# One decoder layer on one core: maxima moved among the projections, layer norm and values on ScalarE, self attention's outputs kept on chip

## The reference

```
x = x + self_attention(layernorm(x))      # causal; values have a bias, the output projection too
x = x + cross_attention(layernorm(x), ctx, mask)   # ctx: (4, 77, 256)
x = x + down(silu(gate(n)) * up(n))       # n = layernorm(x); int32 weights times 1/127, 256 -> 768 -> 256
```

## Time and profile before

| | us |
|---|---|
| median of three runs | 1133.68 |
| the profiled execution | 1134.03 |
| span of its trace | 1132.3 |
| TensorE busy | 1044.6 (92%) |
| VectorE busy | 748.3 (66%) |
| ScalarE busy | 571.1 (50%) |
| GpSimd busy | 224.3 (20%) |
| mean granted TensorE clock | 0.961 of full |

### The profile page before, as it was taken

The page is one execution under the profiler, slowest core; times in us unless marked ns, Lnnn a source line. Parts: engine busy times, 40 slices in busy tenths (PEclk is TensorE's granted clock), DMA queues, the critical chain, the costliest instruction groups (busy, mean ns, idle before and its releaser), DMA issues. The chain is left out here.

```text
span 1132.3 us, 19037 instructions
## 1 busy us (share of the span) xinstructions
PE 1044.6 (92%) x7092; PEld 608.6 (54%) x7092; DVE 748.3 (66%) x1603; ACT 571.1 (50%) x1043; POOL 224.3 (20%) x191
## 2 busy tenths in 40 slices
PE   2888989999999999999999895689989899999997
PEld 2777434444444444444444463344444688888886
DVE  5999887777887887877786374356544555555552
ACT  1445147667776677677666664646646211111110
POOL 6545550000000000000000032600000133333331
PEclk9999779999999999999999996889989899999998
DMA  7259844333334444444020045848774211111101
GB/s 244 104 198 251 248 86 74 73 75 70 71 70 89 90 86 88 89 89 86 23 76 27 35 130 187 204 89 171 169 177 126 80 43 49 51 53 50 48 9 37
DMA packets 89811, 113.66 MB, mean 100 GB/s; under 512 B 13822, under 2 KB 74922, under 8 KB 88183
## 3 DMA queue, kind: packets, MB, share of 16 engines
q1 hardware_dynamic: 86071, 107.43, 38.3%
q10 hardware_dynamic: 3648, 5.02, 2.1%
HBM read 66.26 MB, written 45.45 MB: 99 GB/s over the span
## 5 line engine op out<-in xcount | busy, mean ns | idle before, releaser
L782 ACT ACTIVATE prob<-bank 128x512 f32<-128x512 f32 (+1 forms) x608 | 329.2, 575 | 180.2 <-PE bank L826 101.5
L734 DVE TENSOR_REDUCE pm<-bank 128x1 f32<-128x512 f32 (+3 forms) x608 | 364.3, 655 | 82.5 <-PE bank L810 62.0
L805 PE MATMUL bank<-stk,stq 96*128 96x512 bf16 (+3 forms) x768 | 226.6, 339 | 2.7 <-DVE pm L734 2.1
L822 PE MATMUL bank<-stq,stk 98*128 98x512 bf16 (+3 forms) x768 | 222.4, 328 | 0.9 <-ACT prob L782 0.8
L836 PE MATMUL bank<-prob,va 128*17 128x512 f32 (+3 forms) x1536 | 164.0, 500 | 0.0
L805 PEld LDWEIGHTS bank<-stk,stq 96*128 96x128 bf16 x768 | 70.1, 98 | 153.5 <-DVE pm L734 114.1
L1554 ACT ACTIVATE e_sg<-bank 128x512 f32<-128x512 f32 x48 | 28.7, 598 | 188.7 <-PE bank L135 188.7
L967 POOL TENSOR_TENSOR c_rstd<-c_ve,mhalf 128x4 f32<-128x4 f32 x8 | 8.1, 1010 | 521.3 <-DVE c_ve L128 521.3
L1311 ACT ACTIVATE xprob<-bank 80x512 f32<-80x512 f32 x128 | 72.3, 592 | 65.5 <-PE bank L1349 64.0
L822 PEld LDWEIGHTS bank<-stq,stk 98*128 98x128 bf16 x768 | 69.2, 98 | 56.7 <-issue 12.2
L810 PE MATMUL bank<-tri_q,identb 128*128 128x128 bf16 (+2 forms) x352 | 88.3, 251 | 0.0
(11 more groups left out here) (172 smaller groups left out, 1379.4 us busy)
## 6 DMA issues: line engine op xcount, KB each, us to landing
qk<-a_parts SPq DMA_DIRECT2D x32, 384.0 KB, 4.3
od<-u_out SPq DMA_DIRECT2D x16, 512.0 KB, 3.2
oin<-od SPq DMA_DIRECT2D x32, 256.0 KB
od<-xu SPq DMA_DIRECT2D x16, 512.0 KB, 3.9
xq<-c_parts SPq DMA_DIRECT2D x16, 384.0 KB, 2.9
xstq<-xq SPq DMA_DIRECT2D x32, 192.0 KB, 4.3
stq<-qk SPq DMA_DIRECT2D x28, 192.0 KB, 4.6
stk<-qk SPq DMA_DIRECT2D x14, 384.0 KB, 7.1
```

The costliest lines, as they stand in the source:

```text
L734: nc.vector.tensor_reduce(pm[:, k, h0:h0 + hb, r], src[:, 0:hb * w].rearrange("p (h w) -> p h w", h=hb), AX, ALU.max).then_inc(s_mxe, 1)
L782: nc.scalar.activation(prob[:, U % NPS, 0:hb * n], bank[STB[U % NSB]][:, 0:hb * n], ACT.Exp).then_inc(s_ex, 1)
L805: mm = nc.tensor.matmul(dst[:, h * w:(h + 1) * w], stq[i][0:R, half, h0 + h, r * P:(r + 1) * P], stk[i][0:R, h0 + h, k0:k0 + w], start=(h ...
L822: mm = nc.tensor.matmul(dst[:, h * n:(h + 1) * n], stk[i][0:RM, h0 + h, kt * P:(kt + 1) * P], stq[i][0:RM, half, h0 + h, q0:q0 + n], start ...
```

## The change

In the projections, layer norm moves to ScalarE (scale and a negated mean times scale as bias, which GpSimd computes), the values are evicted by ScalarE without bias into one bank, and the four products share three banks. The value bias goes through the output projection once and into the output bias. In each of chunks 4 to 7, seven units of group 0's maxima are placed among the products (28 of 39 in all, behind the places 0 to 5 that `LEAD_AT` counts), in two other banks. Groups 0 and 1 are loaded one chunk earlier.

In self attention the products of two sets stand together, with 16 buffers of exponentials instead of 12 and three buffers of queries, keys and values instead of four. Each group's outputs and denominators are stored by eight DMAs into tiles on chip (`oall`, `den`), and nothing is read back. In the middle stage these loads are gone, `load_later` comes first, and the feed-forward weights are loaded and converted during cross attention, in 12 pieces.

```diff
-        TB, QKB, VB = (0, 1), (2, 3, 4, 5), (6, 7)
+        TB, QKB, VB = (0, 1), (2, 3, 4), 5
 # SP, chunk(c)
-                if c in (3, 4):
+                if c in (2, 3):
...
+                if c == NCH - 2:
+                    self_rows(sp, 0, 0)
 # GpSimd
             nc.gpsimd.tensor_tensor(rstd[:, c % 2], ve[:, c % 2], mhalf[:], ALU.pow).then_inc(s_pow, 1)
+            g.wait_ge(s_pow, c + 1)
+            nc.gpsimd.tensor_tensor(negm[:, c % 2], mom[:, c % 2, 0], rstd[:, c % 2], ALU.mult).then_inc(s_nm, 1)
 # VectorE
-            normalise1(1)
+            nc.vector.tensor_copy(bvb[:], bv_c[:, :, None].to_broadcast([P, KT, P])).then_inc(s_bvb, 1)
+            lead = iter(range(NLEAD))
             for c in range(NCH):
+                at = LEAD_AT if c >= LEAD_FROM else (0,) * 6
                 split(c, 0)
+                for n in islice(lead, at[0]):
+                    self_item(v, 0, n)
                 split(c, 1)
+                for n in islice(lead, at[1]):
+                    self_item(v, 0, n)
+                if c + 2 < NCH:
+                    stats1(c + 2)
                 if c + 1 < NCH:
                     turned_low(c + 1)
-                if c + 2 < NCH:
-                    stats1(c + 2)
+                for n in islice(lead, at[2]):
+                    self_item(v, 0, n)
                 split(c, 2)
+                for n in islice(lead, at[3] + at[4]):
+                    self_item(v, 0, n)
                 split(c, 3)
-                if c + 2 < NCH:
-                    normalise1(c + 2)
...
+                for n in islice(lead, at[5]):
+                    self_item(v, 0, n)
+            v.wait_ge(s_bo, 1)
+            nc.vector.tensor_tensor(bo_b[:], bank[TB[0]][:, 0:D], bo_b[:], ALU.add).then_inc(s_bob, 1)
 # ScalarE
+            normalise1(1)
             for c in range(NCH):
                 high(c, 0)
                 high(c, 1)
                 middle(c, 0)
                 if c + 1 < NCH:
                     turned(c + 1)
+                middle(c, 1)
+                values_out(c, 0)
                 high(c, 2)
-                middle(c, 1)
+                middle(c, 2)
+                values_out(c, 1)
                 high(c, 3)
-                middle(c, 2)
                 middle(c, 3)
+                if c + 2 < NCH:
+                    normalise1(c + 2)
 # TensorE
+                product(c, 0)
+                for n in islice(lead, at[0]):
+                    self_maxima(t, 0, n)
+                product(c, 1)
...
+                if c + 1 < NCH:
+                    turn(c + 1)
                 values(c, 0)
...
+                product(c, 2)
...
                 values(c, 1)
...
+                product(c, 3)
+                for n in islice(lead, at[5]):
+                    self_maxima(t, 0, n)
 # self attention
-        NPS, LAG, LATE = 12, 3, 3
+        joint_end = [sets[s - s % 2 + 1][3] for s in range(len(sets))]
+        NPS, LAG, LATE = 16, 3, 3
+        LDB = (6, 7)
+        LEAD_FROM, LEAD_AT = 4, (1, 1, 1, 1, 1, 2)
-            plan += [("p", s, 0) for s, x in enumerate(sets) if x[3] - 1 == u - LAG]
+            plan += [("p", s, 0) for s in range(len(sets)) if joint_end[s] - 1 == u - LAG]
 # SP
             def store(g):
+                b, i = g // GB, g % GB
                 sp.wait_ge(s_u, 2 * g + 2)
-                sp.dma_start(od[g:g + 1].rearrange("a h w r t -> (a h w r) t"), u_out[:, g % 2]).then_inc(us[g % 2], 16)
+                for h in range(HG):
+                    row = HD * (HG * (i % 2) + h)
+                    sp.dma_start(oall[row:row + HD, b, i // 2],
+                                 u_out[h * VW:h * VW + HD, g % 2]).then_inc(us[g % 2], 16)
+                    row = S // DT * (HG * i + h)
+                    sp.dma_start(den[row:row + S // DT, b],
+                                 u_out[h * VW + HD:h * VW + VC, g % 2]
+                                 .rearrange("a (c t) -> a c t", t=DT)).then_inc(us[g % 2], 16)
-            for i in range(2, GB):
+            for i in range(2, NB):
                 a.wait_ge(s_set, i + 1)
                 load_self(a, i)
 # middle, SP
-            load_den(sp, B - 1)
-            load_outputs(sp, 3)
-            load_outputs(sp, 4)
+            load_later(sp)
+            store_shares(sp, B - 1)
+            load_shares(sp, B - 1)
             for c in range(NCH):
-                if c + 5 < NCH:
-                    load_outputs(sp, c + 5)
                 for n in range(KT):
                     store_queries(c, n)
-                if c == 0:
-                    store_shares(sp, B - 1)
-                    load_shares(sp, B - 1)
-                    load_later(sp)
-                if c == 4:
-                    load_last_weight(sp)
 # middle, VectorE
+            shares(v, B - 1)
             for k in range(KT):
                 quotients(v, 3, k)
 # middle, ScalarE (and GpSimd's low part likewise)
-                if 3 <= c < 6:
-                    ffn_weight_high(a, c - 3)
 # cross attention, SP
+                if g < 2:
+                    load_weight(sp, g)
+                if g == 6:
+                    load_weight(sp, 2)
 # cross attention, ScalarE
+                    if u == NST2 - 2 and 1 <= g <= 3 * NPC:
+                        ffn_weight_high(a, g - 1)
```

More of the change, by code:

```diff
@@ L1 @@
 from contextlib import ExitStack
+from itertools import islice
 import concourse.bass as bass
@@ L557, in qkv_tensor, with product @@
             t.wait_ge(s_a, 2)
+            def product(c, n):
+                need(t, s_r, 4 * c + n - 2)
+                if c == 0 and n == KT:
+                    t.wait_ge(s_kl, 2)
+                w_ = (wq, wk)[n // KT]
+                m = cut_products(bank[QKB[(4 * c + n) % 3]][:],
+                                 [(w_[:, :, k, (n % KT) * P:(n % KT + 1) * P], xnt[:, c % 2, :, k]) for k in range(KT)])
+                m.then_inc(s_qk, 1)
+            lead = iter(range(NLEAD))
             for c in range(NCH):
+                at = LEAD_AT if c >= LEAD_FROM else (0,) * 6
@@ new lines, in qkv_tensor @@
+                product(c, 2)
+                for n in islice(lead, at[3]):
+                    self_maxima(t, 0, n)
+                values(c, 1)
+                for n in islice(lead, at[4]):
+                    self_maxima(t, 0, n)
+                product(c, 3)
+                for n in islice(lead, at[5]):
+                    self_maxima(t, 0, n)
+            t.wait_ge(s_xt, KT * NCH)
+            t.wait_ge(s_bvb, 1)
+            t.wait_ge(s_later, 16 * 4)
+            for k in range(KT):
+                m = nc.tensor.matmul(bank[TB[0]][:, 0:D], bvb[:, k], wo[:, k], start=(k == 0), stop=(k == KT - 1))
@@ new lines, in self_maxima @@
+        def self_maxima(t, g, n):
+            i, N = g % NB, g * NMX + n
+            kind, m = ring[n]
+            dst = mx_bank(N)
+            if n == 0:
+                t.wait_ge(ld[i], 16 * NLD * (g // NB + 1))
+            need(t, s_mxe, N + 1 - (len(LDB) if g == 0 else NMB))
+            if kind == "t":
+                t.wait_ge(s_mt, 2 * g + m + 1)
+                nc.tensor.transpose(dst[0:32, 0:P // 2].bitcast(BF16),
+                                    mt[:, m].rearrange("p t m -> p (t m)"), identb[:]).then_inc(s_mxf, 1)
+                return
+            half, k, r, h0, hb, k0, w, diag = mx_units[m]
+            for h in range(hb):
+                mm = nc.tensor.matmul(dst[:, h * w:(h + 1) * w],
+                                      stq[i][0:R, half, h0 + h, r * P:(r + 1) * P],
+                                      stk[i][0:R, h0 + h, k0:k0 + w],
+                                      start=(h == 0), stop=not diag, skip_group_check=True)
+            if diag:
+                mm = nc.tensor.matmul(dst[:, 0:hb * w].rearrange("p (h w) -> p h w", h=hb)[:, :, w - P:w],
+                                      identb[:], tri_q[:, 0:hb], start=False, stop=True, skip_group_check=True)
+            mm.then_inc(s_mxf, 1)
@@ L859, in self_tensor @@
                     elif what == "r" and g + ahead < G:
-                        maxima(g + ahead, which)
-            for s, x in enumerate(sets):
-                if x[3] - 1 > NST - 1 - LAG:
+                        self_maxima(t, g + ahead, which)
+            for s in range(len(sets)):
+                if joint_end[s] - 1 > NST - 1 - LAG:
                     products(G - 1, s)
-        ldo = sems("c_ldo", 3)
-        s_den = sem("c_den")
         s_rd = sem("c_rd")
```

326 lines of the change are left out of this document (149 added, 177 removed).

## The result

The changed kernel took 1129.66 us (median of 16 runs) beside 1138.65 us (16 runs) of the kernel before: ratio 0.9928, 95% interval 0.9905 to 0.9952. It is faster, but the forecast was 1099, and the range 1082 to 1118 missed it. The profiled execution took 1128.56 us, its trace spans 1126.8 (before 1132.3). The two traces so differ by 5.4 us where the medians differ by 9.0: the profiled run of the kernel before, at 1134.03, was one of its quicker ones. The table explains the 5.4.

| stretch, from ...

A forecast was written before the change was run, and what follows sets the result against it. It took VectorE to bound the projections, TensorE self attention, and no engine the middle stage. Start +3, self attention -17, middle -23.5 and cross attention +3 made -34.5 us, giving 1099 us, range 1082 to 1118.

The forecast's parts named there:

- -16.6, -4.3 and -2.6: Middle stage: output reads gone -16.6, last chunk's shorter wait -4.3, its products off the low clock -2.6; sum -23.5 us.
- a gain or a loss of 2 is within the bounds: Entry of the middle stage: nothing taken, as quotients wait for eight small stores and shares instead of a store and reads.
- wrong if the middle keeps a wait over 5 us: Middle stage: a sign that would prove the prediction wrong; no wait for outputs was expected there.
- Self attention: -17: Self attention: fewer visits to column tiles save 22 us, banks take back 5; -17 us (-22 to 0).
- The price of a visit: Self attention: going to the column tiles and back costs 0.23 us; 6 visits a group instead of 12 save 1.4 us.
- I take 0.3 us a group: Self attention: loss while eight products run and neither VectorE nor ScalarE gets a bank; 0.3 us a group, 5 us overall.
- The start: +3: Projections up to the first exponentials and group 1's small instructions: +3 us (-6 to +12), last product at 134.0.
- 1.3 us of bounds 0 to 6: Projections, chunk 4: its wait for group 0's load, asked for one chunk earlier behind chunk 2's stores; 1.3 us (0 to 6).
- the same loss that group 0 to 1 has now: Start of self attention: later bias additions meet group 1's small VectorE instructions; two at 2.26 us and the wait, less slack.
- Ten issues at the pitch of rows 5: Before the first exponential: ScalarE's ten DMA issues for group 2 stand ahead of it in its queue; about 5.0 us.
- Rival B: Projections lose more through load and hand-offs: +15 us for +3, giving 1111; chance 0.12.
- Cross attention: +3: Cross attention: twelve weight pieces on ScalarE about nothing, GpSimd idle, three weight loads 1 us each; +3 us (0 to +8).

The follow-up runs named there:

- Experiment 2: Changed kernel, with the last group's eight stores issued first in the middle stage and the last batch element's shares computed after chunk 0's splits: 1121.63 us, ratio 0.9868.
- experiment 1: Changed kernel, with each set's products on their own again, 12 visits to the column tiles per group instead of 6: 1137.72 us, ratio 0.9987.
- experiment 11: Changed kernel, with self attention's products in four visits to the column tiles a group instead of six: 1119.58 us, ratio 0.9842.
- experiment 4: Changed kernel, with chunk 4's seven maxima at later places, none before the second product's transposes: 1130.43 us, ratio 0.9918.
- experiment 13: Changed kernel, with GpSimd's eight bias additions waiting for the last small VectorE casts of groups 0 to 3, two each: 1127.71 us, ratio 0.9902.
- Experiment 14: Changed kernel, with GpSimd's quotients of chunk 0 after its tenth weight piece and group 12's casts, chunk 1's after group 14's casts: 1120.04 us, ratio 0.9851.
- kernel 12: Changed kernel, with last stores in the middle stage, chunk 4's maxima later, GpSimd's bias additions and quotients placed, and four visits a group: 1094.44 us, ratio 0.9621.
- Kernel 10: Changed kernel, with last stores in the middle stage, chunk 4's maxima later, and GpSimd's bias additions and quotients placed by waits on casts: 1108.92 us, ratio 0.9754.
- experiment 5: Changed kernel, with GpSimd's quotients of cross attention and its eight output bias additions cut into quarters: 1132.01 us, ratio 0.9937.
- experiment 3: Changed kernel, with none of group 0's maxima among the projections' products, all 39 following the last product: 1138.98 us, ratio 1.0005.

## Why the prediction was wrong

The forecast's gain of 34.5 us was 9.0 in the medians and 5.4 in the traces. Four terms failed, and self attention's was the largest.

**Middle stage: right.** -16.6, -4.3 and -2.6 make -23.5; measured -24.2. No read of outputs, no wait over 2 us behind the entry, products at TensorE's pace.

**The entry: "a gain or a loss of 2 is within the bounds".** It was +7.5. The prediction had the eight stores at 0.4 us each beside "nothing else" on SP, and looked only at who needs their data. Here an issue took 0.52 to 0.68, 5.1 us in all, and what waited was everybody, because the stage's end waits for SP; in the kernel before the same wait was 0.77 us and invisible. Then the projection of chunk 2 ran at the low clock, 5.78 us where it takes 3.72. By its own sign (wrong if the middle keeps a wait over 5 us) the prediction failed here, with 6.79. Experiment 2 takes it away: 7.0 us for the entry.

**Self attention: -17 was -5.2.** The price of a visit, 0.23 us, was nearly right: counted from the start of each instruction to the start of the next, products fell from 9.34 to 8.60 us a group, and with six leads of 0.09 that is 0.21 a visit. The failed step is "I take 0.3 us a group" for what banks take back. All else in a group (scores, maxima, masks and transposes, without the leads) took 20.03 us before, 20.04 with single sets (experiment 1) and 20.73 in the changed kernel: pairing costs 0.70, in waits of 0.05 to 0.2 us that no list of waits shows. So 1.28 gained less 0.70 is 0.58, where the prediction had 1.4 less 0.3, and the stretch of the table holds 14 of its 16 groups. It is not the length of a burst: with four visits this sum is 20.69 (experiment 11). Why the pairs cost it stays open. The groups with shares cost 0.8 more each where 0.34 was usual, and the last group's tail 1.6.

**The start: +3 was +8.0.** The last product came at 139.1 for 134.0. ScalarE's first eviction started at 38.2 for 37.6, and four chunks took 12.47 for 12.0 each, 1.9 in all: values took 2.15 us for the 1.5 taken from the nearest read of a bank, which fits, though no run shows that this is the reason. Chunk 4 took 18.45 for 15.3, by the load of group 0: the prediction took 1.3 us of bounds 0 to 6, the trace shows 5.34, and experiment 4 gives back 3.5. Chunks 5 to 7 were as forecast or 0.3 shorter. Behind it 39 maxima became 11, as foreseen, and the late bias additions now meet group 1's casts; the prediction named this, and took "the same loss that group 0 to 1 has now". From group 0's to group 1's second transpose it was 32.4 us before and 35.4 after, and experiment 13 puts the additions' part at 3.3. (Ten issues at the pitch of rows 5 are 5.6 us and not 5.0; beside these misses that is small.) Rival B (projections lose 12 more) was the right direction, at 5.

**Cross attention: +3 was +9.7.** The prediction counted the twelve pieces on ScalarE and wrote "GpSimd idles there". It did, but its queue is in order: the two quotients, which started at 828.62 and 849.76 in the kernel before, now stood behind the last piece and ran together over two casts. TensorE waited 4.00 us, and the granted clock was 0.55 in the 7 us behind it. The size is uncertain: the same code took 149.0 to 164.8 us, so +6 to +22 over the one trace before. Experiment 14 removes it by order alone, 9.6 us in the medians, 7.9 between the two traces; the loads are some 2.3.

**A sum that came true elsewhere, in part by luck.** In kernel 12 the stretches of the first table change by +0.6, -16.9, -0.5, -23.1, +0.4 and -1.2, and its 1094.44 us are near the forecast. For the start, the entry and cross attention that is the forecast's mechanism: what stood in front were the late load, the last stores and the places of GpSimd's long instructions. For self attention it is not. Kernel 10, with the forecast's six visits, has -4.9 there; the -16.9 needs the two further visits saved, which the forecast did not have, and the 0.70 us a group are still lost.

## What to carry to other kernels

Before adding an instruction to a queue, ask who waits for the queue and not only who needs the data: the end of a stage waits for all of them, and an in-order queue delays what stands behind. Give GpSimd's long instructions a place between VectorE's small casts, by a wait on the casts' semaphore; cutting them helped with the quotients and made it worse with the bias additions. Where a short wait can be followed by a long stretch at the low clock, compare medians or several traces, since one trace can be off by more than the edit. Where visits to column tiles cost a fixed time, try fewer and longer bursts before fearing for the readers of PSUM.

## What the runs showed of the hardware

- A VectorE cast of 16 columns takes 0.17 us alone, up to 2.27 beside a GpSimd addition or product of 128x1024, and 6.51 beside a run of additions of 128x256 (experiment 5). In experiment 3 additions of 128x1024 also ran back to back, and the cast at 160.15 was let go after 2.27 us, before the run's end. The Trainium skill ("SBUF — State Buffer", Who interferes with whom) says that one holds the shared ports for the whole instruction and the other blocks; that fits 2.27, but the 6.51 goes past one instruction.
- The TensorEngine's switch to column tiles and back costs 0.21 to 0.26 us (1.28 us saved with six visits fewer, 0.51 a group with two fewer), with bursts of 8, 16 and 32 matmuls. The Trainium skill ("TensorEngine Tiling (Array Packing)", Key Properties) names the drain without a price; the traces agree with it and give the price. Of its warning that copies out of PSUM may become the bottleneck (PSUM Bottleneck) no run here shows more than the 0.70 us a group whose cause is open; bursts up to 2.4 us added nothing to it.
- Executions of one kernel differ by the clock they get. Of the changed kernel's, one with a mean granted clock of 0.966 took 1125.5 us and one with 0.956 took 1136.0; of kernel 4's, 0.970 gives 1120.4 and 0.953 gives 1135.8. That is about 1 us for each 0.001, so such differences are larger than most edits here, and an edit of 3 us can only be read in stretches of the trace where both have the same clock.
